# Transformer block on one core: the order of the first loads, of phi's maximum and of the constants is changed

## The reference, cut to what matters

```python
def layernorm(x, eps=1e-05):
    m = jnp.mean(x, axis=-1, keepdims=True)
    v = jnp.var(x, axis=-1, keepdims=True)
    return (x - m) / jnp.sqrt(v + eps)

def attn(x):
    h = layernorm(x) * norm_w + norm_b
    q, k, v = split(einsum('btc,oc->bto', h, qkv_w) + qkv_b)
    o = (q @ k.T / sqrt(C)) @ v
    return x + einsum('btc,oc->bto', o, proj_w) + proj_b

def ffn(x):
    logits = einsum('bmd,dnp->bmnp', x, phi)
    dispatch = softmax(logits, axis=0)
    combine = softmax(logits over n, p)
    slots = einsum('bmd,bmnp->bnpd', x, dispatch)
    y = einsum('bnpd,nde->bnpe', slots, W) + b
    return einsum('bnpd,bmnp->bmd', y, combine)

x = x + layernorm(attn(layernorm(x)))
x = x + layernorm(ffn(layernorm(x)))
```

## Time and profile before

| what | value |
|---|---|
| median of three runs | 641.18 us |
| the profiled execution's own time | 641.88 us |
| its span, first to last instruction | 640.1 us |
| PE busy | 628.2 us (98%) |
| DVE busy | 447.9 us (70%) |
| ACT busy | 359.0 us (56%) |
| POOL busy | 230.2 us (36%) |
| granted TensorE clock, mean | 0.999 |
| moved by DMA | 77.07 MB, mean 120 GB/s |

### The profile page before, as it was taken

How to read it: one execution, slowest core, us unless ns; L and a number is a source line. 1 busy time by engine, 2 the same in 40 slices (tenths; PEclk the granted TensorE clock), 3 DMA queues, 4 the chain that set the end, 5 groups by cost and what they waited for, 6 DMA issues and landing times.

```text
span 640.1 us, 15341 instructions
## 1 busy us (share of the span) xinstructions
PE 628.2 (98%) x5351; PEld 395.4 (62%) x5351; DVE 447.9 (70%) x857; ACT 359.0 (56%) x694; POOL 230.2 (36%) x410
## 2 busy tenths in 40 slices
PE   8999999999999999999999999999999999999996
PEld 8898644545444444444444457777777777777776
DVE  5978888835244453446344399999888888888886
ACT  5666776843233232224444356777777777777764
POOL 5375896820000000000000001555555555555554
PEclk9999999999999999999999999999999999999999
DMA  8920032325766666666555531222222222222201
GB/s 266 402 77 1 1 67 50 67 60 156 201 176 176 177 193 185 173 178 203 135 136 186 159 104 67 91 90 90 90 90 90 90 90 90 90 90 90 90 16 34
DMA packets 78485, 77.07 MB, mean 120 GB/s; under 512 B 6386, under 2 KB 74995, under 8 KB 76147
## 3 DMA queue, kind: packets, MB, share of 16 engines
q1 hardware_dynamic: 76112, 74.48, 38.4%
q10 hardware_dynamic: 2338, 2.16, 1.0%
HBM read 51.71 MB, written 23.07 MB: 117 GB/s over the span
## 4 chain that ended last, share of the span: by engine, by line
PE 79%; DVE 8%; POOL 5%; issue 3%; DMA 2%; ACT 2%; SPq 1%; DVEq 0%; POOLq 0%; ACTq 0%
PE psL L1568 24%; PE psM L1555 11%; PE psL L1687 11%; PE psM L1705 7%; PE psM L1709 7%; PE psM L1706 7%; PE psM L1585 3%; POOL small L492 2%; DMA r_xn<-in_proj_wT 2%; PE psL L1773 1%; PE psL L1453 1%; PE psM L1511 1%; DVE phs L1091 1%; DVE small L1286 1%; DVE r_xn L1305 1%
## 5 line engine op out<-in xcount | busy, mean ns | idle before, releaser
L1568 PE MATMUL psL<-r,r_xn 128*128 128x512 f16 x768 | 176.3, 379 | 0.8 <-DVE r L1112 0.8
L1568 PEld LDWEIGHTS psL<-r,r_xn 128*128 128x128 f16 x768 | 73.4, 98 | 91.0 <-issue 7.0
L762 ACT ACTIVATE r<-psM,small 128x512 f32<-128x512 f32 x64 | 43.7, 682 | 96.3 <-PE psM L1555 95.5
L1555 PE MATMUL psM<-phs,xx 128*128 128x512 f16 (+1 forms) x384 | 93.2, 379 | 0.9 <-DVE xx L1146 0.9
L580 POOL MEMSET r_xn<- 128x8 f16 x2 | 0.3, 137 | 234.2 <-PE psL L1568 234.2
L1110 DVE TENSOR_SCALAR r<-r 128x512 f16<-128x512 f32 x64 | 28.5, 445 | 71.8 <-ACT r L762 71.8
L1687 PE MATMUL psL<-phs,r 128*32 128x512 f16 x1344 | 75.1, 379 | 0.0
L1555 PEld LDWEIGHTS psM<-phs,xx 128*128 128x128 f16 x384 | 37.3, 98 | 45.9 <-DVE xx L1146 1.4
L875 ACT ACTIVATE r<-psL,small 128x512 f32<-128x512 f32 x60 | 41.9, 776 | 37.7 <-DVE small L1313 37.4
L492 POOL TENSOR_TENSOR small<-small,epst 128x2 f32<-128x2 f32 (+3 forms) x75 | 59.8, 797 | 6.2
L1687 PEld LDWEIGHTS psL<-phs,r 128*32 128x32 f16 x1344 | 34.6, 97 | 36.5 <-issue 3.0
(11 more groups left out here) (200 smaller groups left out, 1260.8 us busy)
## 6 DMA issues: line engine op xcount, KB each, us to landing
r<-in_ffn_w SPq DMA_DIRECT2D x23, 1024.0 KB, 5.8
logit_difference<-r SPq DMA_DIRECT2D x256, 64.0 KB, 1.9
xx<-logit_difference SPq DMA_DIRECT2D x16, 1024.0 KB, 4.8
out<-r SPq DMA_DIRECT2D x32, 128.0 KB, 1.7
xres<-in_x SPq DMA_DIRECT2D x7, 512.0 KB, 11.4
r<-in_phi SPq DMA_DIRECT2D x1, 2048.0 KB, 19.3
expert_bias<-r ACTq DMA_DIRECT2D x1, 2048.0 KB, 21.6
r<-expert_bias SPq DMA_DIRECT2D x16, 128.0 KB, 5.5
```

The source lines that it names most:

```text
L1555: ins = mm(bk[j % 2][:, :].rearrange("p (q m) -> p q m", q=EP), xxT[:, 1, j, hx, k, :], phw[:, hp, k, :, bass.ds(nb, 1), :].rearrange("p q ...
L1568: ins = mm(psL[:, i * 512:(i + 1) * 512], x3n[:, b, j, hx, k * P:(k + 1) * P], thl[:, j % 2, hs, :], start=(j == 0 and hx + hs == 0), stop ...
```

## The change

- x comes in eleven groups instead of nine: tiles 0 and 1 alone, then 2 and 3, 4 and 5, 6 and 7 as pairs, the rest in fours. The load of tile 1 is issued by ACT, the others by SP.
- The load of proj_wT (wpT) has a semaphore of its own and is issued behind the first load of batch 1; `weight_scale` waits for four loads, `centre_projection` for the fifth.
- phi's load is issued ahead of the last two loads of x; DVE takes phi's maximum ahead of the last two `stats`, the second of them behind the maximum of the row. `bias_row(0)` goes between the two halves of phi's split.
- On PE `phi_turn` goes ahead of A_step(0), `phi_broadcast` after tile 22.
- On POOL `residual_terms(0)` goes ahead of the terms of batch 1; the f16 identity and `fold_weights` go behind the last `x3_lo`; in `x_terms` the two first steps are next to each other. SP waits for the identity ahead of loads that overwrite it, DVE for the masks.

```diff
--- before.py
+++ after.py
@@ -102,8 +102,10 @@
     TB = 512 // P
     EP = P // Q
     GJ = 4
-    XG = B * NJ // GJ
-    NG = NJ // GJ
+    X_GROUPS = [(0, 0, 1), (0, 1, 1), (0, 2, 2), (0, 4, 2), (0, 6, 2)] + [
+        (b, j, GJ) for b in range(B) for j in range(0, NJ, GJ) if b or j >= 2 * GJ]
+    XG = len(X_GROUPS)
+    NG = XG - NJ // GJ
     assert (B, K, TB) == (2, 2, 4)
 
     x_v = x.rearrange("b (p j) c -> p b j c", j=NJ)
@@ -254,8 +256,8 @@
         bk = [psM[:, i * 512:(i + 1) * 512] for i in range(4)]
 
 
-        par_loaded, rows_loaded = sem("par_loaded"), sem("rows_loaded")
-        x_loaded = [sem(f"x_loaded{g}") for g in range(XG + 1)]
+        par_loaded, rows_loaded, wpT_loaded = sem("par_loaded"), sem("rows_loaded"), sem("wpT_loaded")
+        x_loaded = [sem(f"x_loaded{g}") for g in range(XG)]
         phi_loaded = sem("phi_loaded")
         W_loaded = [sem(f"W_loaded{i}") for i in range(2)]
         pool_const = sem("pool_const")
@@ -314,10 +316,9 @@
         out_stored = [sem(f"out_stored{i}") for i in range(2)]
 
         y_lots = [(1, 0), (1, 1), (0, 0), (0, 1), (1, 2), (0, 2), (1, 3), (0, 3)]
-        N_PAR = 5
-
-
-        X_GROUPS = [(0, 0, 2), (0, 2, 2)] + [(b, j, GJ) for b in range(B) for j in range(0, NJ, GJ) if b + j]
+        N_PAR = 4
+
+
         GROUP_OF = {(b, j + i): g for g, (b, j, n) in enumerate(X_GROUPS) for i in range(n)}
 
 
@@ -351,16 +352,19 @@
                 b, j, n = X_GROUPS[g]
                 sp.dma_start(xres[:, b, j:j + n, :], x_v[:, b, j:j + n, :]).then_inc(x_loaded[g], 16)
 
-            for g in range(NG + 1):
-                load_x(g)
+            for g in range(NG):
+                if g != 1:
+                    load_x(g)
             sp.dma_start(w_raw, qkv_w.rearrange("(s p) c -> p s c", p=P)).then_inc(par_loaded, 16)
             sp.dma_start(wbc, norm_w.rearrange("(o c) -> o c", o=1).broadcast_to([P, C])).then_inc(par_loaded, 16)
             sp.dma_start(bbc, norm_b.rearrange("(o c) -> o c", o=1).broadcast_to([P, C])).then_inc(par_loaded, 16)
             sp.dma_start(qbc, qkv_b).then_inc(par_loaded, 16)
-            sp.dma_start(wpT, proj_wT.rearrange("(k p) e -> p k e", p=P)).then_inc(par_loaded, 16)
-            for g in range(NG + 1, XG + 1):
-                load_x(g)
+            load_x(NG)
+            sp.dma_start(wpT, proj_wT.rearrange("(k p) e -> p k e", p=P)).then_inc(wpT_loaded, 16)
+            load_x(NG + 1)
             sp.dma_start(phf, phi_v).then_inc(phi_loaded, 16)
+            load_x(NG + 2)
+            load_x(NG + 3)
             for w in range(2):
                 sp.dma_start(Wt[:, w], w_v[w]).then_inc(W_loaded[w], 16)
             def store_d(nb, j):
@@ -377,6 +381,7 @@
                 sp.dma_start(by[:, w], b_v[w]).then_inc(b_loaded[w], 16)
             sp.wait_ge(xhalf_done, 1)
             sp.dma_start(Wx, w_v[NT - 1]).then_inc(W2_loaded, 16)
+            sp.wait_ge(ident16_ready, 1)
             for w in range(2):
                 sp.dma_start(byx[:, w], b_v[NT - 2 + w]).then_inc(b23_loaded, 16)
 
@@ -502,9 +507,9 @@
                 if g >= 2:
                     pool.wait_ge(n1_ready, g - 1)
                 own.add(nc.gpsimd.tensor_scalar(e2, mvx[:, b, tn, 1], 1.0 + EPS, EPS * EPS, ALU.mult, ALU.add))
+                own.add(nc.gpsimd.tensor_scalar(nm, mvx[:, b, tn, 0], -1.0, 0.0, ALU.mult, ALU.add))
                 own.wait()
                 own.add(rsqrt(r1[:, b, tn], e2))
-                own.add(nc.gpsimd.tensor_scalar(nm, mvx[:, b, tn, 0], -1.0, 0.0, ALU.mult, ALU.add))
                 own.wait()
                 nc.gpsimd.tensor_tensor(n1[:, b, tn], nm, r1[:, b, tn], ALU.mult).then_inc(n1_ready, 1)
 
@@ -520,13 +525,12 @@
                 own.wait()
                 nc.gpsimd.tensor_tensor(n0[:, b], nm, r0[:, b], ALU.mult).then_inc(r0_ready, 1)
 
-            for g in range(XG + 1):
+            for g in range(NG):
                 x_terms(g)
             residual_terms(0)
+            for g in range(NG, XG):
+                x_terms(g)
             residual_terms(1)
-            pool.wait_ge(r0_ready, 2)
-            nc.gpsimd.tensor_scalar(ident16, ident, 1.0, 0.0, ALU.mult, ALU.add).then_inc(ident16_ready, 1)
-            fold_weights()
 
             def y_terms(b, p):
 
@@ -571,6 +575,9 @@
             x3_lo(0, 4); x3_terms(1, 4); y_terms(0, 7); x3_terms(0, 5); x3_lo(1, 4); x3_terms(1, 5)
             y_terms(1, 6); x3_lo(0, 5); x3_lo(1, 5); x3_terms(0, 6); x3_terms(1, 6); x3_lo(0, 6)
             y_terms(1, 7); x3_terms(0, 7); x3_lo(1, 6); x3_lo(0, 7); x3_terms(1, 7); x3_lo(1, 7)
+            pool.wait_ge(r0_ready, 2)
+            nc.gpsimd.tensor_scalar(ident16, ident, 1.0, 0.0, ALU.mult, ALU.add).then_inc(ident16_ready, 1)
+            fold_weights()
             pool.wait_ge(ry_ready, B * NJ // 2)
             own.add(nc.gpsimd.tensor_tensor(ny.rearrange("p (b j) -> p b j", b=B), n0, ry, ALU.mult))
 
@@ -661,6 +668,7 @@
 
         @block.scalar
         def _(act):
+            act.dma_start(xres[:, 0, 1:2, :], x_v[:, 0, 1:2, :]).then_inc(x_loaded[1], 16)
             act.dma_start(pb_rows[Q - 1:Q], proj_b.rearrange("(o c) -> o c", o=1)).then_inc(rows_loaded, 16)
             act.dma_start(bT[:, :, :], ffn_bT.rearrange("(k p) n -> p k n", p=P)).then_inc(rows_loaded, 16)
 
@@ -1009,6 +1017,7 @@
 
             def centre_projection():
 
+                dve.wait_ge(wpT_loaded, 16)
                 own.add(V.tensor_reduce(wm, wpT, AX_X, ALU.add))
                 own.wait()
                 own.add(V.tensor_scalar(wm, wm, 1.0 / C, None, ALU.mult))
@@ -1038,21 +1047,16 @@
                 own.wait()
                 V.tensor_tensor(w_aug[:, :, C - 1], bcol, qbc, ALU.add).then_inc(wprime_ready, 1)
 
-            stats(0)
-            stats(1)
-            stats(2)
-            stats(3)
-            stats(4)
+            for g in range(NG):
+                stats(g)
             proj_bias()
             weight_scale()
-            stats(5)
+            stats(NG)
             own.add(V.tensor_reduce(bmx, bT.rearrange("p k n -> p (k n)"), AX_X, ALU.max, apply_absolute_value=True))
             bias_columns()
             primed_weights()
             centre_projection()
-            stats(6)
-            stats(7)
-            stats(8)
+            stats(NG + 1)
 
             def pow2_scale(i, top, least, done):
 
@@ -1068,9 +1072,10 @@
             dve.wait_ge(phi_loaded, 16)
             V.tensor_reduce(pm[:, 0:1], phf.rearrange("p k n -> p (k n)"), AX_X, ALU.max,
                             apply_absolute_value=True).then_inc(phi_max, 1)
-            bias_row(0)
+            stats(NG + 2)
             dve.wait_ge(phi_row, 1)
             V.tensor_reduce(gm[0:1, 0:1], bk[0][0:1, 0:P], AX_X, ALU.max).then_inc(phi_top, 1)
+            stats(NG + 3)
             dve.wait_ge(phi_spread, 1)
             pow2_scale(0, bk[0][:, C:C + 1], 2.0 ** -100, phi_scale)
             dve.wait_ge(phi_scale, 1)
@@ -1085,6 +1090,7 @@
             for k in range(K):
                 for src, c in phi_quadrants(k):
                     own.add(V.tensor_scalar(phs[:, 0, k, c].rearrange("p (t c) -> p t c", c=Q), src, sg[:, 0:1], None, ALU.mult))
+            bias_row(0)
             own.wait()
             for k in range(K):
                 for src, c in phi_quadrants(k):
@@ -1203,6 +1209,7 @@
                 own.wait()
                 own.add(V.tensor_reduce(top4[:, EP:EP + 1], topT, AX_X, ALU.max))
                 own.wait()
+                dve.wait_ge(fold_const, 1)
                 V.tensor_scalar(top4[:, 0:EP], fmask[:, :, 0], top4[:, EP:EP + 1], None, ALU.mult).then_inc(top_masked, 1)
 
             def top_scale(folded):
@@ -1525,10 +1532,9 @@
                 if t == NJ + 3:
                     R_step(0)
                 if t == NJ + 5:
+                    phi_turn()
                     A_step(0)
                 if t == NJ + 6:
-                    phi_turn()
-                if t == NJ + 8:
                     phi_broadcast()
             pe.wait_ge(phi_scale, 1)
             def turn_xd(p):
```

## The result

| | before | changed |
|---|---|---|
| median of the comparison's runs | 641.18 us (640.64 to 641.63, 7 runs) | 643.86 us (642.11 to 644.95, 7 runs) |
| the profiled execution | 641.88 us | 642.99 us |
| its span | 640.1 us | 641.0 us |

A forecast was written before the change was run, and what follows sets the result against it. TensorE (PE) was taken as the bound, with waits of 1.73 us in three places. Gains of 0.4 + 0.22 + 0.36 = 0.98 us off the median 641.18 gave 640.2 us, with an 8-in-10 range of 639.1 to 641.2.

The forecast's parts named there:

- phi's landing: PE at phi_turn, ahead of A_step(0): every microsecond of phi landing past 29.4 costs one, 642.8 us at 33; chance 0.04.
- the one on POOL: POOL ahead of tile 16's terms: residual_terms(0), 3.6 us, fills a pause of 6.29 us; cost 0.
- The swapped pair in `x_terms`: The two first steps of x_terms on POOL: in order on one engine, cost 0.
- First loads, 0.4: PE at tiles 4 and 5: smaller groups let ACT start sooner, gain 0.2 to 0.46 us, taken as 0.4.
- one of the signs of being wrong: Listed signs: PE pausing ahead of A_step(0), tile 2 waiting for ACT, or the late stretch changing by over 0.5 us.
- The doubt about two queues: First loads of x: two queues save only issue time, so tile 0 lands no sooner than 3.84; gain 0.2 us.
- The weight load, 0.22: PE at tiles 15 and 16: DVE's weight step goes sooner, so S_copy(0) starts at 23.55, not 23.77; gain 0.22 us.
- Phi and the last products, 0.36: PE at h_pair(1, 0): DVE, ahead by 1.9 us, does bias_row(1) before PE asks; the 0.36 us wait goes.
- More comes back later: Rival, 0.32: part of PE's 3.46 us standing between 74.54 and 108.03 returns; a third to a half gives 639.1 to 638.6.

## Why the prediction was wrong

It gave 640.2 us, 639.1 to 641.2, and 0.04 for slower. The measured 643.86 lies 2.7 us outside. The one rival on the slower side, phi's landing, has no part in it.

**The step that failed** is the one on POOL: "residual_terms(0) (3.6 us) fills a pause of 6.29 ahead of tile 16's terms", costed at 0. Three things are wrong in it. The first and the third had their numbers in the text; for the second no row of before shows a held step.

- The pause was read from before, where it began at 14.24. The same prediction cut the first eight tiles into five groups, priced a group of one at 1.3 us and one of two at 1.45 (1.46 and 1.60 in the trace), and never carried that chain on to where the pause begins. By its own prices that is 4.57 + 2 × 1.3 + 3 × 1.45 + 2 × 1.75 = 15.0; it was 16.1, behind the start of DVE's product. The swapped pair in `x_terms`, costed at 0 as well, is part of it: a group of four takes 1.94 us (12.27 to 14.21) where it took 1.84, a group of two 1.60 where it took 1.54. No run takes the swap out alone.
- The 3.6 us were right as work (3.8 in the kernel with the move alone). In place of the change they took 5.32, because one step was held by DVE. Behind them, tile 16's own terms were held by 1.5 more. Nothing was asked about who else used the memory in this stretch, though DVE's product at 16.96 stood in the earlier trace rows. This is the item that decides: with the same late pause and the same 3.8 us but without the holds the kernel takes 640.37.
- The other end of the pause moves as well. The term of the weight load was to bring tile 16's statistics sooner, so the pause closes from both sides.

**First loads, 0.4.** The pair with `residual_terms(0)` at its old place measures 0.36 us by the medians. In the profiled execution of the changed kernel the term was nothing (tile 5 at 12.53 against 12.51). Two steps of its working were off. POOL's groups cost 0.15 us more each than given, so that ACT starts on tile 4 at 10.63 and not at 10.0 to 10.4. And tiles 2 and 3 were not ready before PE: it waits 0.46 us for tile 2, one of the signs of being wrong that the forecast named. What sets the pace is DVE's first read of x and POOL's chain behind it. In the six kernels with the small groups tile 5 starts 8.78 to 8.82 us behind that read, whether the warm-up ends at 6.62 (here) or at 7.98 (with DVE's products in six). The doubt about two queues was right; with one queue the first tile was read sooner still.

**The weight load, 0.22.** In before tile 17 starts 2.67 us behind tile 15; in the kernel with `residual_terms(0)` back it is 2.44 (22.35 to 24.79), so the size is right. Its cause is not shown. The kernel with the move of `residual_terms(0)` alone and the one with phi's part alone have the load at its old place and 2.44 as well, with DVE's product at 15.76 and 16.64 and not at 16.96; the kernel with all first loads from SP has it moved and 2.70, with the product at 16.58. Alone the moved load is not to be told from nothing.

**Phi and the last products, 0.36.** No wait at `phi_turn`; phi landed 17.1 us after its issue, at 26.2, at the early end of 25.7 to 29.7, and its maximum ran 26.91 to 31.30. In the changed kernel all behind it is shifted by the 2.57 us. Where that is undone, the scales start at 37.64 (37.4 was given), the split ends at 47.72 (47.65), and `h_pair(1, 0)` has no wait: 24 pieces follow one another in 5.34 us from 54.24, while with the weight load alone 24 take 5.74, which hides the same 0.4 us that was read as 0.36 in before. The size is right. The reason given for it was not whole, as phi's part alone shows.

**The sum.** 640.2 us is what the change makes without the one move, 640.25 measured, and with the move one group later, 640.14; against before on the same chip these are gains of 0.86 and 0.84 us. Without the first loads' part it is 641.11 − 640.61 = 0.50, where 0.22 + 0.36 = 0.58 was given. So 0.98 was a fair sum of the parts on PE's path, and the error lies in the one part that was costed at nothing. That the time comes within 0.05 is in part luck: two of the three terms rest on waits that come and go from one profile to the next.

**More comes back later.** Between 74.54 and 108.03 PE of the changed kernel is busy for 31.79 us, where it was 30.03. That looks like this rival, but the window cuts other work, since everything is 2.57 us later: in 108.03:166.00 PE is busy for 57.17 us, where it was 57.97. Over both stretches it is 88.96, against 88.94 to 88.97 in the three kernels that differ from before or from the changed kernel only in where `residual_terms(0)` stands. The eleven experiments show 30.96 to 31.18 in the first stretch, among them those that are the same as before in time. What none of them has is this wait of before, which leaves before 88.00, in the profiled execution that lies 0.70 us over its median:

```profile
91.11 1.47 PE L1555 MATMUL psM<-phs,xx 128*128 128x512 f16 x6 [0.92 <-DVE xx L1146]
```

Whether the kernel before always has it can't be said from one profile of it. The largest gain of all, 641.09 − 639.98 = 1.11 us, is hardly over the forecast's 0.98, so this rival did not come true.

## What to carry to other kernels

A pause on a helper engine is only a price of nothing if both its ends are read in the new order: take every change of the same edit to that engine's queue, add up the times to the moment in question, and compare with when the next step is due there. Put work into such a pause behind the step that is due, not ahead of it: the same block costs nothing one group later. And look at what the other engines do in that stretch, not only at this one: a step of 0.2 us became one of 1.7 because of DVE's instruction beside it.

## What the runs showed of the hardware

- A small POOL instruction that reads SBUF and starts while DVE multiplies 128x1536 f32 from two SBUF inputs (1.76 us) ends 0.06 to 0.07 us after DVE: 1.60 to 1.81 us instead of 0.2 when it starts right behind DVE, 1.01 and 1.11 when it starts 0.81 and 0.71 behind. A memset took its 0.11. A root of 1.01 us, in the kernel with `residual_terms(0)` back, took 2.51 and ended 0.87 behind DVE's product, which began at 14.55:

```profile
14.67 2.51 POOL L497 TENSOR_TENSOR small<-small,epst 128x4 f32<-128x4 f32 x1
```

- What counts is that POOL's step begins behind DVE's. A root of POOL that was already running when DVE's product began kept its 2.90 us, and the product its 1.76; the steps behind the product's start are the ones held.
- Cut into six instructions, the product costs DVE 2.12 us, and POOL's small steps beside it take 0.25 to 0.32 us instead of 0.2.
- A first load of 128 KB with a second one on ACT's queue was read hardly sooner than 256 KB on SP's (3.60 to 3.87 against 3.68 to 3.93), while with both on SP's, one behind the other, it was read at 3.33, in one profile.
- The 28 warm-up pieces of PE took from 4.72 us (the changed kernel) to 6.08 (with DVE's products in six), with a granted clock of 1.00 in the rows of both. From 2.90 on they come at 7 or 8 a microsecond in both. In the short one there are 12 in the microsecond from 4.90, in the long one 7 and then 6. Why the pace changes at 4.90 in one execution and not in the other isn't shown.
